# A graph network of four blocks on one core: row fetch on ScalarE's queue, three sums begun early, node types as a product, first operands made in the preparation

## The chip, the cores and the metric

The kernel runs on one core of one Trainium2 chip. The metric is the device time of the whole kernel in microseconds, one launch with all weights read from HBM. Three runs of the kernel before took 1722.24, 1723.06 and 1729.78 us; the median is 1723.06 us.

## What is computed

625 nodes with 768 features, 10625 edges (two directions of 5000 random pairs, and a loop per node), all in float32. Four blocks follow each other, and each one adds to `x` what it computes from `h = max(layernorm(x), 0)`:

```python
# L0: relational mean over 34 edge types, then a GCN layer
mean = agg.reshape(34, n, -1) / max(cnt, 1)
h1 = einsum('rni,rio->no', mean, W_rel) + h @ W_root + b_rgcn
x = x + gcn(h1, W_gcn, b_gcn)
# L1: two GCN layers with relu between
x = x + gcn(relu(gcn(h, W1, b1)), W2, b2)
# L2: three relational layers with 3 edge types; the first has 768 + 128 inputs and 896 outputs
h = concat([h, node_emb[node_type]], -1)          # node_emb is 3 x 128
h = relu(rgcn(h, w_rel1, w_root1, b1)); h = relu(rgcn(h, w_rel2, ...)); h = relu(rgcn(h, w_rel3, ...))
x = x + h
# L3: one GCN layer
x = x + gcn(h, W, b)
```

`gcn` multiplies rows by a weight matrix and sums them over edges with the factor `dinv[src] * dinv[dst]`. `rgcn` multiplies by one matrix for each edge type, sums over the edges of the type, divides by their number, and adds a product with a root matrix.

## The kernel before

**Precision.** Each float32 operand of a large product is held as two fp32r parts, a high one (ScalarE casts it) and a low one (VectorE subtracts the high one from the original), and a product is three matmuls: high by high, high by low, low by high. So each operand passes ScalarE, then VectorE, then TensorE. Nodes lie as 5 tiles of 125 partitions; features as chunks of 128.

**Three programs in a row**, with a barrier of all engines between them (`clear`, L62 to L64):

1. `prepare` sorts the edges by type into units of three tiles of 128 slots, with one-hot matrices on VectorE and matmuls that count on TensorE. Beside that it normalises `x` (`statistics`, L88 and `row_scales`; the activation L1245) and makes `h @ W_root` in 60 float32 matmuls (`root`, L1518), which TensorE works off where its own counting waits: 8, then 4 after each of 5 groups of slots (6 after the last), and so on; what is left runs at the end. ScalarE takes each half tile of them (`take`, L1258), and GpSimd adds them to `sums` in HBM by an indirect DMA (L1221) for four of the five node tiles, and then waits until these have landed. SyncE loads the first unit's weights into `w_raw`.
2. `add_means` runs over some 33 units. Per unit GpSimd gathers rows into `e_raw` (L1895), VectorE makes the matrix `pick` (L2180), ScalarE and VectorE split rows and weights (L1975, L2186, L1979, L2191), TensorE sums (L2328) and multiplies (L2344), ScalarE scales the result (L2014) and GpSimd adds it to `sums` (L1907). In units 6 to 25 the adjacency counts of block L2 are made beside it. After the last unit VectorE adds up the counts of the three edge types (L2246, L2249), then all engines run one pass of a loop that is there for keys with more edges than fit (L2262 and after; PE L2292, L2300). SyncE stores its counts (L1877).
3. `load_rows` and `layers`. SyncE fetches the 625 rows of `sums` in 6 column chunks of 12 DMAs (L128); ScalarE turns the counts into fp32r (`a`, L144), VectorE scales a chunk by `dinv` (L155), ScalarE and VectorE split it. Then come the layers `l0b`, `l1a`, `l1b`, `l21`, `l22`, `l23`, `l3`. A GCN layer is six sums over edges (`edge_sums`, L741, 20 matmuls of 316 columns each) into two banks of PSUM, each then split by ScalarE (L405) and VectorE (L527), and then five products (`products`, L770, 36 matmuls of 384 columns per node tile). A sum may only start in a bank whose sum before has been split (`free`). Between two layers the products' tiles are taken, normalised and split one by one: VectorE L537, L88, L97 to L81, L548; ScalarE L417 casts the high part from `h`; VectorE L559 makes the low part. The next layer's first two sums are begun with four node tiles each and ended with the fifth (`sums_of_all`).

**Layer l21** multiplies 7 feature chunks: 6 of `h` and one of the node type's embedding, which `embeddings()` has written beside `h` in 15 vector instructions. Its rows are turned with 7 transposes per tile (L800), split (L421, L576), and multiplied for 3 edge types and 5 node tiles with 42 matmuls of 448 columns (L770), and for the root matrix with 7 outputs of 42 matmuls of 316 columns (`root_columns`, L845). Weights come through a ring of 4 buffers: the load of a fifth chunk waits until VectorE has split the first (`w_ready`, L520). After the weights of the first edge type, VectorE's program takes and normalises the last tile of l1b (L537 to L554) and then enters `kind_products`, whose first step is L582.

## Time and profile before

| | |
|---|---|
| median of three runs | 1723.06 us |
| the profiled execution | 1722.8 us, of which the span of instructions is 1720.8 us |
| TensorE busy | 95% of the span |
| VectorE, ScalarE, GpSimd | 57%, 36%, 19% |
| mean granted TensorE clock | 0.961 of full |
| DMA | 227.65 MB, 132 GB/s over the span |

The page also cuts the span into 40 slices of 43 us:

```
PE   6987999989999999999498999999999999999988
PEclk7868999999999999999699999999999999999989
DMA  7305997867997789894632131231222212221101
```

Each digit is a busy share in tenths, and PEclk the granted clock in tenths of full speed. The preparation is in the first three to four slices, the means up to slice 19, the layers behind it. A matmul's own duration includes its way through the array, so successive ones overlap; what one costs is read from a run of many, its length divided by their number.

### The profile page before, as it was taken

The numbers are of one execution on the slowest core, as the hardware profiler recorded it, in microseconds if no ns is written. First come the engines' busy times: TensorE is split into PE (matmuls) and PEld (weight loads), VectorE is DVE, ScalarE is ACT, GpSimd is POOL, SyncE is SP. The second block draws the span as 40 slices with busy tenths as digits, with TensorE's granted clock in tenths as the row PEclk, the third lists the DMA queues.
The fourth block names the chain that finished last, engine by engine and source line by source line (L and its number), as shares of the span: only waits on it lengthen the run. The fifth ranks groups of instructions, "written<-read, shape, count | busy, mean of one in ns | idle before, by whom it ended". The sixth has DMA issues, their size and how long they took to land. (4 is left out here: it accounts for less than half of the span.)

```text
span 1720.8 us, 28124 instructions
## 1 busy us (share of the span) xinstructions
PE 1627.5 (95%) x9970; PEld 1510.7 (88%) x9971; DVE 982.0 (57%) x1488; ACT 614.0 (36%) x823; POOL 327.7 (19%) x293
## 2 busy tenths in 40 slices
PE   6987999989999999999498999999999999999988
PEld 4766888879999999988498999999999999999988
DVE  8775997866776676564565474245253442423372
ACT  5104655545665556554222223112231221312220
POOL 0203544543344444342200000000010000000000
PEclk7868999999999999999699999999999999999989
DMA  7305997867997789894632131231222212221101
GB/s 231 90 10 148 258 254 215 241 199 206 271 246 212 211 243 282 250 261 106 106 88 65 42 104 50 63 94 33 56 65 83 75 37 83 74 56 56 55 28 45
DMA packets 97975, 227.65 MB, mean 132 GB/s; under 512 B 11986, under 2 KB 37700, under 8 KB 97898
## 3 DMA queue, kind: packets, MB, share of 16 engines
q1 hardware_dynamic: 72525, 152.19, 27.9%
q0 software_dynamic: 21488, 71.97, 18.7%
q10 hardware_dynamic: 3885, 2.41, 0.5%
q8 instruction: 56, 0.92, 0.2%
q14 instruction: 21, 0.17, 0.0%
HBM read 187.13 MB, written 41.29 MB: 133 GB/s over the span
## 5 line engine op out<-in xcount | busy, mean ns | idle before, releaser
L770 PE MATMUL layers_ps_o<-layers_w_hi,layers_g_hi 128*125 128x384 f32 (+1 forms) x900 | 237.6, 345 | 2.6 <-DVE layers_w_lo L520 2.5
L2344 PE MATMUL l_means_ps<-l_means_w_hi,l_means_g_hi 128*128 128x512 f32 (+1 forms) x912 | 237.8, 342 | 2.1 <-DVE l_means_g_lo L2202 2.0
L770 PE MATMUL layers_ps_o<-layers_w_lo,layers_g_hi 128*125 128x384 f32 (+1 forms) x900 | 237.1, 344 | 0.0
L1979 ACT CAST l_means_w_hi<-w_raw 128x768 fp32r<-128x768 f32 x204 | 170.1, 838 | 187.5 <-PE l_means_ps L2344 168.5
L770 PE MATMUL layers_ps_o<-layers_w_hi,layers_g_lo 128*125 128x384 f32 (+1 forms) x900 | 236.8, 344 | 0.0
L2344 PE MATMUL l_means_ps<-l_means_w_hi,l_means_g_lo 128*128 128x512 f32 (+1 forms) x912 | 235.0, 339 | 0.0
L2344 PE MATMUL l_means_ps<-l_means_w_lo,l_means_g_hi 128*128 128x512 f32 (+1 forms) x912 | 234.1, 338 | 0.0
L2191 DVE TENSOR_TENSOR l_means_w_lo<-w_raw,l_means_w_hi 128x768 fp32r<-128x768 f32 x204 | 186.2, 947 | 69.7 <-ACT l_means_w_hi L1979 60.5
L2328 PE MATMUL l_means_ps<-l_means_pick,l_means_e_hi 128*128 128x256 f32 (+1 forms) x612 | 166.3, 302 | 17.4 <-DVE l_means_e_lo L2186 10.8
L582 DVE TENSOR_TENSOR h_lo<-layers_ps_o,h_hi 125x768 fp32r<-125x768 f32 (+1 forms) x45 | 45.1, 1001 | 238.0 <-ACT h_hi L426 238.0
L741 PE MATMUL layers_ps_g<-a,h_hi 125*128 125x316 f32 x630 | 151.2, 323 | 29.4 <-DVE h_lo L163 12.4
L2344 PEld LDWEIGHTS l_means_ps<-l_means_w_lo,l_means_g_hi 128*128 128x128 f32 x912 | 153.4, 188 | 20.5
L2344 PEld LDWEIGHTS l_means_ps<-l_means_w_hi,l_means_g_hi 128*128 128x128 f32 x912 | 152.0, 189 | 21.6 <-DVE l_means_w_lo L2191 1.8
L2344 PEld LDWEIGHTS l_means_ps<-l_means_w_hi,l_means_g_lo 128*128 128x128 f32 x912 | 153.8, 188 | 19.5
L770 PEld LDWEIGHTS layers_ps_o<-layers_w_hi,layers_g_hi 128*125 128x125 f32 x900 | 162.2, 185 | 7.8 <-DVE layers_w_lo L520 2.9
L1907 POOL DMA_INDIRECT sums<-l_means_y,l_means_row_now x76 | 130.2, 1713 | 201.7 <-ACT l_means_y L2014 173.0
L770 PEld LDWEIGHTS layers_ps_o<-layers_w_hi,layers_g_lo 128*125 128x125 f32 x900 | 163.5, 185 | 4.0
L770 PEld LDWEIGHTS layers_ps_o<-layers_w_lo,layers_g_hi 128*125 128x125 f32 x900 | 163.4, 185 | 3.9
L2328 PE MATMUL l_means_ps<-l_means_pick,l_means_e_lo 128*128 128x256 f32 (+1 forms) x612 | 164.6, 299 | 0.2 <-issue 0.2
L741 PE MATMUL layers_ps_g<-a,h_lo 125*128 125x316 f32 x630 | 149.2, 319 | 0.0
L2202 DVE TENSOR_TENSOR l_means_g_lo<-l_means_ps,l_means_g_hi 128x512 fp32r<-128x512 f32 (+1 forms) x126 | 78.1, 636 | 121.6 <-ACT l_means_g_hi L1993 115.5
L741 PEld LDWEIGHTS layers_ps_g<-a,h_hi 125*128 125x128 f32 x630 | 111.3, 200 | 33.6 <-issue 12.9
(329 smaller groups left out, 2356.7 us busy)
## 6 DMA issues: line engine op xcount, KB each, us to landing
w_raw<-in_L_gnn_W_rel SPq DMA_DIRECT2D x204, 384.0 KB, 6.7
layers_w_raw<-in_L_gnn_w_rel SPq DMA_DIRECT2D x39, 384.0 KB
layers_w_raw<-in_L_gnn_w_rel SPq DMA_DIRECT2D x21, 448.0 KB
layers_a_raw<-adj SPq DMA_DIRECT2D x9, 769.0 KB
layers_w_raw<-in_L_gnn_W SPq DMA_DIRECT2D x18, 384.0 KB
list_now<-targets SPq DMA_DIRECT2D x33, 192.0 KB
layers_w_raw<-in_L_gnn_w_root SPq DMA_DIRECT2D x13, 384.0 KB
layers_w_raw<-in_L_gnn_w_root SPq DMA_DIRECT2D x7, 448.0 KB
```

Of the source, the lines that this page charges most:

```text
L582: v.tensor_tensor(in_halves(h_lo[:, k, 0:layer.width]), out_rows(bank, layer.width), in_halves(h_hi[:, k, 0:layer.width]).bitcast(F32), AL ...
L741: mm = t.matmul(ps_g[:, buf % 2, at:at + PART[p]], rows[:, k, f * 128:(f + 1) * 128], a[:, k, cols], start=(k == 0 and i == 0), stop=(k == ...
L770: mm = t.matmul(ps_o[0:NP, i % 2, a_half, 0:half], g[:, f, at], part_of_w[:, f, a_half * half:(a_half + 1) * half], start=(f == 0 and g is ...
L1907: nc.gpsimd.indirect_dma_start(out=sums, in_=y[:, j, :], in_offset=None, compute_op=ALU.add, out_offset=bass.IndirectOffsetOnAxis(ap=row_n ...
L1979: nc.scalar.copy(w_hi[:, f, :], w_raw[:, f, :]).then_inc(w_hi_ready, 1)
L2191: v.tensor_tensor(w_lo[:, f, :], w_raw[:, f, :], w_hi[:, f, :].bitcast(F32), ALU.subtract)\
L2202: v.tensor_tensor(g_lo[:, f:f + per, at], sums_in_bank(f // per, tiles), g_hi[:, f:f + per, at].bitcast(F32), ALU.subtract).then_inc(g_rea ...
L2328: mm = t.matmul(sums, e[:, j, f * 128:(f + 1) * 128], pick[:, j, 0:cols], start=(j == 0 and part == 0), stop=(j == UNIT - 1 and part == 1))
L2344: mm = t.matmul(ps_y[j][:, o0:o1], g[:, f, at], w[:, f, o0:o1], start=(f == 0 and opens and g is g_hi and w is w_hi), stop=(f == fc - 1 an ...
```

## The change

- **Rows.** SyncE's 12 DMAs (L128) are gone. At the end of `add_means` GpSimd signals `all_added` when the last scatter has landed; ScalarE waits for that and issues 8 DMAs (column chunks 0, 1, 2 to 3, 4 to 5, two partition groups each) from its own queue, still inside `add_means`. `load_rows` casts `a` tile by tile, with the first rows between, and TensorE waits tile by tile; 8 matmuls of a 128 x 128 identity run first (`AWAKE`), and 12 at the end of `add_means` (`LAST_WARM`).
- **Third sum.** GCN layers begin three sums before the fifth tile is there; the third lies in the odd output bank (`gcn_bank`). The fifth tile is split in columns 0 to 255 and the rest. ScalarE computes the high part from `x` with scale and bias (`shift`), beside VectorE's `h`.
- **Node types.** The embedding chunk of `h` becomes 35 columns: one-hot at 0 to 2 and again at 32 to 34. TensorE multiplies the embedding's high and low part by the chunk's weights (`typed_rows`, 6 matmuls for each of 4 weight matrices); ScalarE (`typed_rows_high`) and VectorE (`typed_rows_low`) write high and low parts into `w_lo`, and the chunk's share of a product is one matmul instead of three. Its weights are loaded first, its product comes last, but first for the fifth tile.
- **Preparation.** The statistics of 4 of 5 tiles move to ScalarE (three activations each) and the scales behind the first rank copy; the cast of the diagonal moves to GpSimd; 16 + 4 matmuls keep TensorE busy; 6 instead of 8 root matmuls at first; `pick`, `e_hi`, `e_lo` of unit 0 are made here; GpSimd no longer waits for its scatters, `add_means` waits for all 5. The first unit's weights are loaded later, since their buffer now holds one-hots first.
- **Adjacency.** The adds L2246 to L2249 move from behind the last unit to before the loop of the last units.

```diff
@@ load_rows
-                sp.dma_start(chunk(h[part], f), chunk(rows[part], f)).then_inc(loaded[f], 16)
-        nc.scalar.preload_act_table(ACT.Sqrt)
-        nc.scalar.copy(a[:], adj_all[:]).then_inc(a_ready, 1)
+        copy_counts(0)
+        act.wait_ge(rows_ready, 1)
+        nc.scalar.copy(chunk(h_hi, 0), chunk(h, 0)).then_inc(hi_ready, 1)
+        for k in range(1, NT):
+            copy_counts(k)
...
@@ layers, ScalarE and VectorE
-                    nc.scalar.activation(h_hi[:, k, 0:dim], h[:, k, 0:dim], ACT.Relu).then_inc(layer.hi_ready, 1)
+                    for part in parts_of(k):
+                        nc.scalar.activation(h_hi[:, k, part], x[:, k, part], ACT.Relu, bias=shift[:, k:k + 1],
+                                             scale=rstd[:, k:k + 1]).then_inc(layer.hi_ready, 1)
...
+            if not relu:
+                v.scalar_tensor_tensor(shift[:, at], moments[:, at, 0], -1.0, rstd[:, at], ALU.mult, ALU.mult)\
+                    .then_inc(layer.rows_ready, len(group))
...
+        def typed_rows_high(w):
+            act.wait_ge(typed_summed, typed_number(w) + 1)
+            nc.scalar.copy(in_halves(typed[:, 0:w.width]), typed_bank(w)).then_inc(typed_high, 1)
+        def typed_rows_low(w):
+            n = typed_number(w)
+            dve.wait_ge(typed_high, n + 1)
+            low = in_halves(typed[32:HOT, 0:w.width])
+            v.tensor_tensor(low, typed_bank(w)[32:HOT], low.bitcast(F32), ALU.subtract).then_inc(typed_ready, 1)
...
         def kind_products(layer, r):
+            if layer is l21:
+                typed_rows_low(layer.w[r])
@@ layers, TensorE
+        def typed_rows(w):
+            pe.wait_ge(w_ready, w.first + 1)
+            for i, (e, part_of_w) in enumerate(((0, w_hi), (0, w_lo), (1, w_hi))):
+                for a_half in range(2):
+                    mm = t.matmul(typed_bank(w)[:, a_half, :], emb_parts[e],
+                                  part_of_w[:, w.fc - 1, a_half * half:(a_half + 1) * half], start=(i == 0), stop=(i == 2))
+            mm.then_inc(typed_summed, 1)
...
+                    if by_type and f == w.fc - 1:
+                        pe.wait_ge(typed_ready, typed_number(w) + 1)
+                if by_type and f == w.fc - 1:
+                    terms = ((g_hi[0:HOT, f, at], typed),)
...
+            sums_of_all(layer.w.fc, 3, gcn_bank, free, wait_rows, layer.g_summed)
@@ prepare
-            pool.wait_ge(first_gathered, 16 * UNIT)
-            pool.wait_ge(root_added, 16 * (NT - 1))
-            s.copy(diagonal_keys, diagonal[:].unsqueeze(2).broadcast_to([types, types, EC])).then_inc(diagonal_ready, 1)
+            g.tensor_copy(diagonal_keys, diagonal[:].unsqueeze(2).broadcast_to([types, types, EC])).then_inc(diagonal_ready, 1)
+            for k in range(1, NT):
+                s.activation(h[:, k, 0:width], x[:, k, :], ACT.Copy, accum_out=totals[:, k:k + 1]).then_inc(summed_rows, 1)
...
+                s.activation(h[:, k, 0:width], x[:, k, :], ACT.Square, bias=minus_mean[:, k:k + 1],
+                             accum_out=squares[:, k:k + 1]).then_inc(squared, 1)
...
+            act.wait_ge(first_gathered, 16 * UNIT)
+            for j in range(UNIT):
+                s.copy(e_hi[:, j, :], e_raw[:, j, :]).then_inc(first_split, 1)
...
-            root(8)
+            root(6)
@@ add_means
-            pool.wait_ge(root_added, 16)
+            pool.wait_ge(root_added, 16 * NT)
...
+            act.wait_ge(all_added, 1)
+            for i, (f0, f1) in enumerate(ROW_PARTS):
+                for part in (slice(0, 112), slice(112, NP)):
+                    nc.scalar.dma_start(to[part, :, f0 * 128:f1 * 128], summed_rows[part, :, f0 * 128:f1 * 128])\
+                        .then_inc(second.rows_loaded[i], 16)
```

## Rows read from the trace of the kernel before

**Rows 1.** The page, part 1: TensorE's busy time, share of the span, instructions.

```profile
PE 1627.5 (95%) x9970; PEld 1510.7 (88%) x9971; DVE 982.0 (57%) x1488; ACT 614.0 (36%) x823; POOL 327.7 (19%) x293
```

**Rows 2.** Waits of TensorE by line and releaser: us in total, times, longest us.

```profile
PE layers_ps_g L741 <- DVE h_lo L163: 12.4, 1, 12.4
PE l_means_ps L2328 <- DVE l_means_e_lo L2186: 10.8, 1, 10.8
PE layers_ps_g L741 <- DVE h_lo L559: 8.5, 4, 3.2
...
PE layers_ps_g L741 <- DVE layers_g_lo L527: 6.2, 4, 3.5
PE l_means_ps L2328 <- issue: 5.6, 2, 5.4
```

**Rows 3.** The chain that ended last, in order of time: start us, us, what.

```profile
881.63 19.00 PE layers_ps_o L770 x108
...
924.21 14.61 PE layers_ps_g L741 x80
...
1035.02 8.62 PE layers_ps_o L770 x42
...
1306.79 36.57 PE layers_ps_g L845 x252
```

**Rows 4.** A stage: us, busy us of PE, PEld, DVE, ACT, POOL, PEclk, DMA, GB/s.

```profile
924.20:930.00 5.80, 5.79 (x22) 5.79 (x23) 2.42 (x3) 1.29 (x3) 0.00 (x0) 0.50 0.63 175
```

**Rows 5.** Timeline at the preparation's end: start, us, instruction [idle before <- releaser].

```profile
127.51 1.99 POOL L1221 DMA_INDIRECT sums<-h_rows,node_rows  x1 [31.21 <-ACT h_rows L1258]
...
134.48 0.48 ACT L1258 COPY h_rows<-prep_ps 125x384 f32<-125x384 f32 x1 [3.39 <-PE prep_ps L1518]
...
139.86 1.28 ACT L1969 ACT_TABLE_LOAD   x1 [4.90 <-PEq L64]
...
145.23 0.68 PE L2328 MATMUL l_means_ps<-l_means_pick,l_means_e_hi 128*128 128x384 f32 x1 [10.79 <-DVE l_means_e_lo L2186]
```

**Rows 6.** The instructions of line L1221: time from issue to landing.

```profile
DMA to landing us min/median/max: 9.7/10.4/14.5
```

**Rows 7.** GpSimd: a line's durations (ns min/median/max), and a cast in the timeline.

```profile
L1892 POOL COPY l_means_src_now<-s_src_index x33: 185/317/5081, 145.2 to 771.8; 128x3 int32 x31, 128x3 int32<-128x3 int32 x2
...
848.46 0.29 POOL L135 CAST layers_ones<-layers_ones_f 125x128 fp32r<-125x128 f32 x1
```

**Rows 8.** Timeline at the end of the means, all engines.

```profile
817.83 1.79 DVE L2246 TENSOR_TENSOR adj_all<-l_means_cnt 125x3150 uint16<-125x3150 uint16 x1
...
823.94 0.21 DVE L2262 TENSOR_SCALAR l_means_rank<-l_means_rank 125x85 f32<-125x85 f32 x1 [1.36 <-issue]
...
827.13 0.47 POOL L1900 COPY l_means_row_now<-s_row_index 128x3 int32 x1 [6.11 <-DMA sums<-l_means_y,l_means_row_now]
...
833.73 3.58 PE L2292 MATMUL l_means_ps<-e_raw,l_means_again_slot 125*128 125x240 f16 x17 [4.79 <-DVE e_raw L2157]
...
834.07 1.53 POOL L1907 DMA_INDIRECT sums<-l_means_y,l_means_row_now  x1 [0.30 <-issue]
...
844.63 0.36 SPq L1877 DMA_DIRECT2D adj<-l_means_cnt  x1
```

**Rows 9.** Timeline at the start of the layers.

```profile
848.14 6.65 SPq L128 DMA_DIRECT2D h_rows<-sums  x12
...
849.44 2.82 ACT L144 CAST a<-adj_all 125x3150 fp32r<-125x3150 uint16 x1
...
855.84 0.87 PE L741 MATMUL layers_ps_g<-a,h_hi 125*128 125x316 f32 x2 [12.43 <-DVE h_lo L163]
```

**Rows 10.** Timeline: VectorE's low part of the fifth tile behind l0b.

```profile
920.72 0.96 DVE L559 SCALAR_TENSOR_TENSOR h_lo<-h_rows,h_hi 125x768 fp32r<-125x768 f32 x1 [0.91 <-ACT h_hi L417]
```

**Rows 11.** Timeline at the start of l21: TensorE's seventh chunk, VectorE's L582.

```profile
1032.78 0.67 PE L770 MATMUL layers_ps_o<-layers_w_hi,layers_g_hi 128*125 128x448 f32 x2 [0.74 <-DVE layers_w_lo L520]
...
1037.57 1.08 DVE L582 TENSOR_TENSOR h_lo<-layers_ps_o,h_hi 125x896 fp32r<-125x896 f32 x1
```

384 lines of the change are left out of this document (250 added, 134 removed).

## Prediction

> **What bounds the kernel now.** First the page's busy times: TensorE is busy 95% of the span [rows 1], so a gain is either matmuls that go or the 5% in which it waits, together with the slow clock behind such waits. Then TensorE's waits by releaser [rows 2]. They are few and long: 12.4 us before the layers' first sum, 10.8 us before the first unit, 8.5 us for normalised tiles, 6.2 us for a freed bank. Then the chain of waits, for what one matmul costs back to back at full clock [rows 3]: 19.00 / 108 = 0.176 us with 384 columns, 8.62 / 42 = 0.205 with 448, 36.57 / 252 = 0.145 with 316. Last the granted clock: it stood at 0.50 (1.2 GHz of 2.4) for 5.8 us from 924.2 on, behind two waits [rows 2, 4]. Its four sums of 80 matmuls took 14.61 us [rows 3] where 80 x 0.145 = 11.6 would do, so such a pair of waits costs 3.0 us beyond itself.
>
> All terms are against the profiled execution: 1722.8 us, a span of 1720.8 us and 2.0 us around it. The median of the runs is 0.3 us higher, so I use the same number for both.
>
> **1. Preparation and first unit.** GpSimd issues its fourth scatter at 127.51 [rows 5], and it lands 9.7 to 14.5 us later [rows 6]. That is about 138, and the barrier opens at 139.86, though ScalarE's last take ends at 134.96 [rows 5]. Without the wait the takes set the end. Two root matmuls more stand at the tail, about 1.3 us, and the chain before it is about 1.2 us shorter (root(6) lets the slot counts go 1.2 us earlier, and VectorE loses four tiles of statistics), so the end stays near 135.2 and the block opens at about 136.1: -3.75. ScalarE's 12 new activations lie in a stretch where it waited; VectorE's pick and e_lo of unit 0 lie beside the tail of root matmuls, which hides them. TensorE started its first unit at 145.23, 5.4 us after the block opened [rows 5], because pick, e_hi and e_lo came first. These are made already, so it can start about 1.3 us after. ScalarE's and VectorE's splits of the weights, which stood behind them, become late next: the sixth sum waits about 0.7 us for them. That leaves -3.15. Sum **-6.9**, bounds -3 (splits and first gather late) and -8. The means run on TensorE, so the shift should stay.
>
> **2. Adjacency adds.** The adds and the entry to the pass take VectorE from 817.83 to 823.94 [rows 8]. Before the loop of the last units they hold up VectorE's split of the next unit's first sums: about 5 us of work against the 4.2 us that TensorE's sums last. **+0.5**, bounds 0 and +2.
>
> **3. End of the means and l0b.** TensorE's part of the pass started at 833.73 after 4.79 us of waiting for VectorE [rows 8]. Without the adds it starts when the last unit is done and its loop is entered, about 830.5, and the store of the counts (844.63) comes out near 839.5. Now ScalarE is late next. The last scatter is issued at 834.07 to 835.6; the one before it held GpSimd 6.1 us after its issue [rows 8], so `all_added` comes at about 841.9. Eight DMAs at 0.45 us (12 took 5 to 6.65 us on SyncE [rows 9]) are 3.7 us more, and a barrier of 0.9 us follows: the layers open at about 846.8 instead of 848.14. **-1.3**, bounds +1.5 and -4.
> In the layers TensorE began 7.7 us after the opening, at 855.84 [rows 9]: DMA, scaling, a 2.8 us cast of all counts [rows 9], two splits. Now the first rows have landed before the block, and scaling, cast and split of one chunk are 3 x 0.8 us: it starts at +2.6. The weights of l0b no longer queue behind 12 row DMAs, so the 3.5 us wait of the third sum [rows 2] goes, and a third bank lets ScalarE and VectorE lag one sum. VectorE's 24 steps of some 0.77 us are then 18.5 us from +0.1, about as long as the six sums, 6 x 20 x 0.147 = 17.6. With 1.8 us at the slow clock and 0.3 us of small waits the products start at +22.3, where before they started at 881.47 (six matmuls ahead of the chain's piece at 881.63 [rows 3]), +33.3. **-11.0**, bounds -6 (rows or weights land late, slow clock) and -14.
>
> **4. Third sum and split behind a normalisation.** Behind l0b: per tile VectorE loses the 0.91 us wait for ScalarE [rows 10] and gains the shift (0.2 us) and a smaller wait, -0.46 per tile. Over tiles 2 to 4, with the fifth in two parts, the first part of the last tile is ready at about 919.5 instead of 921.7. TensorE has 48 matmuls (7.0 us) until 920.1 instead of 32, so its waits of 0.4 and 3.2 us go, the wait for a bank shrinks from 1.0 to 0.5, and the slow clock's 3.0 us go with them [rows 2 to 4]: the sums end at 931.2 instead of 938.8, **-7.6**, bounds -4.5 and -8. Behind l1a only a part of one bank wait (1.3 us) goes: **-0.85**. Behind l23 VectorE's tile takes longer than TensorE's product, so it stays late: waits of 2.2, 2.7 and 0.6 us become about 1.4, 0.8 and 0.8, and half the slow clock stays: **-5.7**, bounds -3 and -7.5.
>
> **5. Node types (l21).** Removed: 4 of 42 matmuls in 15 products, 60 x 0.205 = 12.3 us, and 28 x 0.145 = 4.1 us in the root. Added: 24 typed matmuls, 4.9 us. For edge types 1 and 2 all of it counts, since the splits of the typed rows hide behind 36 matmuls of the first tile: 2 x (1.23 - 4.1) = -5.7. Edge type 0 is another matter. Its weights come in at VectorE's pace, the last chunk at 1032.78 [rows 11], so the first tile ends its six plain chunks at about 1034.0. Its typed product then waits for `typed_rows_low`, which in VectorE's program stands behind the last tile's normalisation, where L582 stood, at 1037.57 [rows 11]. 1.08 us for it, taken from L582's row of the same width: 1038.7. **A new wait of 4.7 us**, and the slow clock behind it, 2.2 us (less than the 3.0 above). Against that stand 3 x 0.82 us of tiles 1 to 3. Tile 4 and the root's first output are paced by VectorE's reciprocal and splits, which shift along, with a second wait of about 1 us for the root's typed rows and 0.9 us of other waits and slow clock; then six outputs save 0.58 us each. Type 0 and root together: 4.7 + 2.2 + 0.35 (the later chunk order) - 2.45 + 1.9 - 3.5 = +3.2. Sum **-2.5**, bounds -8 (typed rows in time) and +3 (slow clock twice).
>
> Embedding loads (GpSimd's two DMAs), 35 columns instead of 128, SyncE's later load of the first weights (its buffer is free at about 82, needed at 137) and the warming matmuls cost nothing: they lie where the engine has nothing due.
>
> **Sum:** -6.9 + 0.5 - 1.3 - 11.0 - 7.6 - 0.85 - 5.7 - 2.5 = -35.35. 1722.8 - 35.35 = **1687.5 us**.
>
> **Rivals.**
> (a) The typed rows come in time, or the clock does not fall behind them: term 5 is -9. 1681 us. Against it: the order in VectorE's program.
> (b) The rows' early fetch brings little. ScalarE issues it so late that block and rows come as before, and only the smaller cast and the third bank count: terms of part 3 are +1 and -6. 1694 us. For it: the estimate has the fetch only 6 us ahead of the old one, and ScalarE holds the barrier.
> (c) GpSimd's cast of 2890 columns blocks VectorE's compare of the types (L1299), which all of the preparation waits for. At 0.29 us for 128 columns [rows 7] it takes 4 to 6.5 us from 2.7 on, and the compare began at 5.5: +1.5 to +3.8, 1690 us. The rows show the other direction only: a copy of three columns on GpSimd took 185 ns to 5081 ns [rows 7]. The Trainium skill, "SBUF — State Buffer", section "Who interferes with whom", says that a VectorE instruction with two inputs in SBUF and a GpSimd one that reads SBUF exclude each other for a whole instruction, and the first to start wins. By that rule the cast wins here, and the time is that of (c); the trace agrees as far as GpSimd's waits go, and has no long GpSimd instruction that could show VectorE waiting.
> (d) Slower than before. TensorE once waited 5.4 us in the means for nothing that the profile shows [rows 2], on entering a new loop. If that is the loading of its program, the change, which adds branches to straight code of the layers and another order to each program, could bring more such pauses. With the slow clock one costs 5.4 + 2.2 = 7.6 us; from five new ones on the gain of 35 is gone: 1724 us and above. Against it: the layers' code, straight already, shows no such wait.
>
> **Chances.** Forecast (1681 to 1694 around 1687.5) 0.58; (a) 0.13; (b) 0.15; (c) 0.08; (d) 0.02; the rest, 0.04, lies between 1700 and 1723. The range must reach (a), (b) and (c) with the bounds of the large terms: 1676 to 1700. About 0.5% is what a measurement can tell from no change. Faster by over 0.5% (below 1714.4) 0.95, within 0.5% 0.03, slower 0.02.
>
> **What the changed profile would show.** The means' first matmul at about 137.4; ScalarE's row DMAs from about 835 (842 less the shift of 6.4); TensorE's first sum 2.6 us after the layers open and the products 22 us after; no wait over 1 us between the products of l0b and l1a; a wait of 4 to 5 us for `typed_ready` in the first tile of l21 and a clock of 0.50 behind it; the count of 448-column matmuls on L770's line down by 60, with 24 typed ones on a line of their own. I would be wrong by much if the means absorbed the early start, which a first matmul at 137 with an unchanged end of the means would show, or if the rows' DMAs were issued after the barrier's other engines had come.

## The result and the profile after

The changed kernel takes 1708.1 us (1701.5 to 1709.1) against 1724.0 us, a ratio of 0.988 (95% interval 0.986 to 0.991). It is faster, by less than half of what was forecast (1687.5, range 1676 to 1700). In the profiled executions the span went from 1720.8 to 1707.2 us, 13.6 less, where the sum had 35.4. Two executions beside these, one of 4007.7 us in `fetch_sync` below and one of 2369.7 us of the kernel before, are left out of all times and ratios. The page, part 1:

```profile
PE 1628.4 (95%) x9954; PEld 1498.6 (88%) x9955; DVE 981.2 (57%) x1486; ACT 626.3 (37%) x858; POOL 333.3 (20%) x297
```

There are 16 matmuls fewer than in [rows 1], and the busy time is the same. So what is gained is waiting, and not much of it. The waits of TensorE, after (line and releaser: us in total, times, longest):

```profile
PE l_means_ps L2497 <- issue: 18.3, 5, 7.0
PE layers_ps_o L1019 <- PEq L64: 6.6, 1, 6.6
PE prep_ps L1684 <- DMA prep_root_w<-in_L_gnn_W_root: 5.9, 1, 5.9
...
PE layers_ps_o L871 <- DVE layers_w_lo L644: 4.6, 1, 4.6
...
PE l_means_ps L2513 <- DVE l_means_g_lo L2373: 3.6, 2, 2.7
PE layers_ps_g L821 <- DVE h_lo L626: 2.5, 2, 1.9
PE layers_ps_g L821 <- DVE layers_g_lo L591: 2.4, 4, 0.7
```

Against [rows 2]: the 12.4 us for the first rows' low part are a 6.6 us wait for the block; 8.5 and 6.2 us for normalised tiles and a freed bank are 2.5 and 2.4. Those parts did what they should. New are 18.3 us of "issue" where there were 5.6, and waits for the root weights (2.6 before), for `g_lo` and for the typed rows. By stages, each bounded by the same matmuls in both traces:

| stage | us before | after | forecast | measured |
|---|---|---|---|---|
| A: to the first matmul of the means | 145.2 | 144.3 | -6.9 | -0.9 |
| B: means, to the end of the last unit | 683.5 | 692.1 | +0.5 | +8.5 |
| C: to l0b's products | 52.9 | 40.7 | -12.3 | -12.2 |
| D: to the end of l1a's sums | 57.2 | 50.1 | -7.6 | -7.1 |
| E: to the end of l1b's sums | 50.5 | 49.9 | -0.85 | -0.6 |
| F: l21, to l22's root | 317.5 | 321.8 | -2.5 | +4.3 |
| G: to l3's products | 374.2 | 367.9 | -5.7 | -6.3 |
| H: to the end | 39.8 | 40.4 | 0 | +0.7 |

C, D, E and G are within 0.6 us of the forecast. A, B and F hold 20.8 of the 21.8 us that are missing. The 0.7 us that part 1 of the forecast gave to late splits fall into unit 0 and so into stage B.

One profile of each kernel says less of A and F than of the rest. Over all the profiled executions below, the means began at 144.4 to 147.6 us in four with the preparation of before, and at 141.7 to 144.4 in eight with the changed one: some 3 us earlier on average, not 0.9. Stage F took 316.6 to 319.4 us in those four and 319.3 to 322.6 in the ten that keep the changed l21.

### The profile page after: what moved, and what is told of

Read it like the earlier page. It is cut to its first block and busy times, and to the rows that moved or that the text cites. A ratio compares the mean times of both kernels' runs of the same rounds, so it can differ in the third digit from the quotient of the medians.

```text
span 1707.2 us, 28150 instructions
## 1 busy us (share of the span) xinstructions
PE 1628.4 (95%) x9954; PEld 1498.6 (88%) x9955; DVE 981.2 (57%) x1486; ACT 626.3 (37%) x858; POOL 333.3 (20%) x297
## 3 DMA queue, kind: packets, MB, share of 16 engines
q0 software_dynamic: 21552, 71.98, 18.7%
## 5 line engine op out<-in xcount | busy, mean ns | idle before, releaser
L871 PE MATMUL layers_ps_o<-layers_w_lo,layers_g_hi 128*125 128x384 f32 (+2 forms) x900 | 239.4, 347 | 4.6 <-DVE layers_w_lo L644 4.6
L871 PE MATMUL layers_ps_o<-layers_w_hi,layers_g_hi 128*125 128x384 f32 (+1 forms) x870 | 230.5, 346 | 0.8 <-DVE layers_w_lo L584 0.8
L871 PE MATMUL layers_ps_o<-layers_w_hi,layers_g_lo 128*125 128x384 f32 (+1 forms) x870 | 228.6, 344 | 0.0
L2497 PE MATMUL l_means_ps<-pick,e_hi 128*128 128x256 f32 (+1 forms) x612 | 167.7, 304 | 18.8 <-issue 18.3
L871 PEld LDWEIGHTS layers_ps_o<-layers_w_lo,layers_g_hi 128*125 128x125 f32 (+1 forms) x900 | 162.7, 186 | 12.4 <-DVE layers_w_lo L644 4.9
L2497 PE MATMUL l_means_ps<-pick,e_lo 128*128 128x256 f32 (+1 forms) x612 | 165.6, 300 | 0.0
L871 PEld LDWEIGHTS layers_ps_o<-layers_w_hi,layers_g_hi 128*125 128x125 f32 x870 | 156.5, 186 | 8.5 <-issue 3.4
L821 PE MATMUL layers_ps_g<-a,h_hi 125*128 125x316 f32 x590 | 136.0, 312 | 7.1 <-DVE h_lo L626 2.5
L2497 PEld LDWEIGHTS l_means_ps<-pick,e_hi 128*128 128x128 f32 x612 | 119.7, 196 | 22.1 <-issue 19.8
L2064 POOL DMA_INDIRECT e_raw<-rows,l_means_src_now x99 | 127.0, 1283 | 49.5 <-POOL l_means_src_now L2061 27.2
```

Of the source, the lines that this page charges most:

```text
L821: mm = t.matmul(to[:, at:at + PART[p]], rows[:, k, f * 128:(f + 1) * 128], a[:, k, cols], start=(k == 0 and i == 0), stop=(k == NT - 1 and ...
L871: mm = t.matmul(ps_o[0:NP, i % 2, a_half, 0:half], g, part_of_w[:, a_half * half:(a_half + 1) * half], start=(f == order[0] and n == 0), s ...
L2064: nc.gpsimd.indirect_dma_start(out=e_raw[:, j, :], out_offset=None, in_=rows, in_offset=bass.IndirectOffsetOnAxis(ap=src_now[:, j:j + 1], ...
L2497: mm = t.matmul(sums, e[:, j, f * 128:(f + 1) * 128], pick[:, j, 0:cols], start=(j == 0 and part == 0), stop=(j == UNIT - 1 and part == 1))
```

## Where the three stages lost it

**Preparation (A).** Its end and the first matmul of the means, after (timeline: start, us, instruction, [idle before <- releaser]):

```profile
137.33 0.48 ACT L1409 COPY h_rows<-prep_ps 125x384 f32<-125x384 f32 x1 [3.39 <-PE prep_ps L1684]
142.41 1.28 ACT L2139 ACT_TABLE_LOAD   x1 [4.60 <-PEq L64]
...
144.33 0.68 PE L2497 MATMUL l_means_ps<-pick,e_hi 128*128 128x384 f32 x1 [7.04 <-issue]
```

ScalarE's last take ends at 137.81 and the block opens 4.60 us later. In [rows 5] it was 134.96 and 4.90 us. The row's releaser, TensorE's sequencer (PEq L64), only takes part in the barrier. What comes last is GpSimd's fourth scatter, still, though the program no longer waits for it (timeline, and time from issue to landing):

```profile
130.36 1.99 POOL L1367 DMA_INDIRECT sums<-h_rows,node_rows  x1 [29.55 <-ACT h_rows L1409]
...
DMA to landing us min/median/max: 10.6/10.6/10.6
```

It lands at 140.94, and the block opens 1.47 us behind that. The trace has GpSimd's closing DRAIN, the instruction with which it leaves the block, from 130.11 to 141.28: it ends 0.34 us behind the landing. So the wait that was removed stands in this instruction as well. In the kernel before the scatter landed at 137.87 and the block opened 1.99 us behind it.

And the takes end 2.85 us later than before, not 0.2. TensorE's start in the preparation, after:

```profile
34.40 6.89 PE L1684 MATMUL prep_ps<-prep_root_w,prep_root_g 128*125 128x384 f32 x12 [5.88 <-DMA prep_root_w<-in_L_gnn_W_root]
41.13 2.91 PE L1694 MATMUL prep_ps<-prep_is_tile,w_raw 125*128 125x186 f16 x34
...
44.08 1.29 DVE L1526 TENSOR_TENSOR prep_is_slot<-prep_iota,prep_slot_of 125x2176 f16<-125x2176 f16 x1 [6.61 <-PE prep_ps L1694]
```

The same in the kernel before:

```profile
33.60 5.42 PE L1518 MATMUL prep_ps<-prep_root_w,prep_root_g 128*125 128x384 f32 x16 [2.60 <-DMA prep_root_w<-in_L_gnn_W_root]
```

VectorE was 4.1 us ahead at its first one-hots (26.4 against 30.5), but TensorE reached `root` sooner only to wait longer for its weights, which land at 34.4 instead of 33.6. After 5.88 us of idling its 12 root matmuls take 0.57 us each, before 16 took 0.34 (the trace shows each of the kernel's 6 and 8 as two). The slot counts, for which VectorE and all behind it wait, begin at 41.1 instead of 38.9. Both times vary: the weights landed at 33.0 to 34.3 in the four executions of before and at 33.5 to 34.6 with the changed preparation, the takes ended at 134.3 to 137.3 and at 135.3 to 138.0. So the lead of 4.1 us is lost in each of them, and of the 2.85 us about 1 is the change, by the averages, and the rest differs from execution to execution.

**Means (B).** Time from the first matmul of one unit to that of the next, units counted from 0, for all those that differ by over 0.5 us:

| unit | 0 | 2 | 3 | 5 | 6 | 7 | 10 | 11 | 26 | 30 |
|---|---|---|---|---|---|---|---|---|---|---|
| before | 26.8 | 17.6 | 17.9 | 25.3 | 19.8 | 18.7 | 24.4 | 20.4 | 17.3 | 17.7 |
| after | 27.8 | 21.5 | 16.9 | 27.4 | 25.4 | 20.5 | 18.8 | 18.1 | 21.5 | 16.9 |

Unit 26 is the one beside which VectorE does the adjacency adds now. After:

```profile
673.27 1.12 DVE L2415 TENSOR_TENSOR adj_all<-adj_all,ident 125x125 uint16<-125x125 uint16 x5
...
676.66 0.69 DVE L2373 TENSOR_TENSOR l_means_g_lo<-l_means_ps,l_means_g_hi 128x512 fp32r<-128x512 f32 x1 [2.27 <-ACT l_means_g_hi L2161]
...
677.48 0.61 PE L2513 MATMUL l_means_ps<-l_means_w_hi,l_means_g_hi 128*128 128x512 f32 x2 [2.72 <-DVE l_means_g_lo L2373]
```

The adds begin at 669.61. ScalarE's half (`g_hi`) had been there since 674.07, before the adds ended: the 2.27 us between them and `g_lo` are VectorE's own, in which the trace shows it load bounds from memory, enter the loop and branch. I had counted the adds, 5 us against 4.2, and not the entry. TensorE waits 2.7 us and the unit costs 4.2 us.

The other units hold pauses of TensorE for which the profile names nothing. After:

```profile
193.77 0.58 PE L2497 MATMUL l_means_ps<-pick,e_hi 128*128 128x256 f32 x1 [2.73 <-issue]
...
273.41 0.38 PE L2497 MATMUL l_means_ps<-pick,e_hi 128*128 128x256 f32 x1 [1.92 <-issue]
...
298.76 0.58 PE L2497 MATMUL l_means_ps<-pick,e_hi 128*128 128x256 f32 x1 [6.40 <-issue]
```

Before:

```profile
368.61 0.58 PE L2328 MATMUL l_means_ps<-l_means_pick,l_means_e_hi 128*128 128x256 f32 x1 [5.41 <-issue]
```

The one of before, in front of unit 11, is gone, and three others are there: in unit 2, and in front of units 6 and 7. By the kernel, units 2, 6, 11 and 26 are the first of a loop of TensorE's, and unit 7 is the second pass of one. Units 2 to 11 together cost 4.4 us more. In these pauses the DMA view shows the queue that carries instructions at work. After, 292.5 to 298.7 (packets, MB, share of 16 engines):

```profile
q8 instruction: 2, 0.03, 1.9%
```

and before, 363.3 to 368.6:

```profile
q8 instruction: 1, 0.02, 1.2%
```

The changed kernel's second execution (below) has no pause in front of unit 7. From the start of unit 6 to that of unit 7 the same row reads, in the first (273.5 to 298.7) and in the second (270.7 to 289.3):

```profile
q8 instruction: 4, 0.07, 0.9%
...
q8 instruction: 2, 0.03, 0.6%
```

Two packets fewer, and no pause. Elsewhere such packets move without one, at 378.8 and 387.0 for instance.

**l21 (F).** The wait for the typed rows came where it was forecast, for 4.56 us, and the granted clock of 1025 to 1030 was 0.51, that is 1.2 GHz of 2.4:

```profile
1023.94 1.08 DVE L644 TENSOR_TENSOR layers_w_lo<-layers_ps_g,layers_w_lo 3x896 fp32r<-3x896 f32 x1
...
1025.08 1.10 PE L871 MATMUL layers_ps_o<-layers_w_lo,layers_g_hi 35*125 35x448 f32 x2 [4.56 <-DVE layers_w_lo L644]
...
1025.00:1030.00 5.00, 4.92 (x16) 4.08 (x17) 2.06 (x3) 1.85 (x3) 0.00 (x0) 0.51 0.00 0
```

That part was right. What was not is the saving. Typed matmuls within an undisturbed tile, TensorE's matmuls and its weight loads (PEld), after:

```profile
1148.62 0.56 PE L871 MATMUL layers_ps_o<-layers_w_hi,layers_g_lo 128*125 128x448 f32 x2
1149.11 0.67 PE L871 MATMUL layers_ps_o<-layers_w_lo,layers_g_hi 35*125 35x448 f32 x2
1149.71 0.68 PE L871 MATMUL layers_ps_o<-layers_w_hi,layers_g_hi 128*125 128x448 f32 x2
1150.23 0.56 PE L871 MATMUL layers_ps_o<-layers_w_lo,layers_g_hi 128*125 128x448 f32 x2
...
1149.11 0.29 PEld L871 LDWEIGHTS layers_ps_o<-layers_w_lo,layers_g_hi 35*125 35x125 f32 x2 [0.30 <-issue]
1149.71 0.29 PEld L871 LDWEIGHTS layers_ps_o<-layers_w_hi,layers_g_hi 128*125 128x125 f32 x2 [0.31 <-issue]
```

A pair of 128-row matmuls stands 0.40 us behind the last one. Into and out of the pair with 35 rows it is 0.49, 0.60 and 0.52: the weight load starts 0.30 us late both times, where loads of equal rows run on without a gap. A tile of 36 plain and 2 typed matmuls takes 8.22 us (1140.89 to 1149.11), where 38 x 0.205 is 7.8. Against the 8.62 us of [rows 3] that saves 0.40 us per tile, half of the 0.82 forecast.

## The experiments

All kernels compute the full result. In the expectations a pause "at unit 11" is the one in front of it. Theory A, in the three runs after the first, is the account above. The changed kernel itself once more, to see what repeats:

> The changed kernel once more, nothing edited. Its first profile shows TensorE paused four times in the means with nothing that the profile shows ahead of it (2.7 us in the third unit, 1.9 before the seventh, 6.4 before the eighth, after 7.0 before the first), where the kernel before had one such pause (5.4 us, before the twelfth unit). Theory P (place): the pauses belong to places of TensorE's program, which the change has shifted, and come back at the same units with about the same lengths; the unit from 172.1 us on and the loop of the keys repeat within 0.2 us. Theory R (chance): they belong to what the DMA engines carry in that execution; they lie at other units or have lengths that differ by microseconds, and the whole time moves with their sum. Time 1701 to 1709 us by both.

1707.0 us (1694.7 to 1709.5), ratio 0.990. The profiled execution took 1694.7 us, the others 1705 to 1710. It had the pauses of units 2 and 6 (theory P) but not that in front of unit 7, and so spent 664.6 us from the first matmul to unit 33 instead of 675.0. It also had its first matmul at 141.87, so 2.5 us of stage A vary between executions. I compare stages and not only times below.

**Typed rows at full height.** The same number of matmuls, with 128 rows, the unused ones zero:

```diff
-                    terms = ((g_hi[0:HOT, f, at], typed),)
+                    terms = ((g_hi[:, f, at], w_lo[:, f, :]),)
-                        terms = ((typed[:, out_chunk], g_hi[0:HOT, f, :]),)
+                        terms = ((w_lo[:, f, out_chunk], g_hi[:, f, :]),)
```

> Node types: the chunk of the node type stays one matmul instead of three, but with all 128 rows (rows 35 to 127 of the left operand are zero) instead of 35. In the changed kernel a tile of l21 took 8.22 us for 38 matmuls, where 38 x 0.205 = 7.8 were forecast; before and behind each pair with 35 rows 0.50 and 0.60 us pass instead of 0.41. Theory B: the cost lies in the chunk's place or its own operand (the typed rows in the low weights): a tile stays at 8.2 us and the time at the changed kernel's.

1698.1 us, ratio 0.984 (0.981 to 0.987). l21 took 312.4 us instead of 321.6, 9.2 less (and 7 to 10 less than in the other executions that keep the changed l21), and a tile 7.76 us:

```profile
1143.68 0.57 PE L871 MATMUL layers_ps_o<-layers_w_lo,layers_g_hi 128*125 128x448 f32 x2
...
1151.44 0.56 PE L871 MATMUL layers_ps_o<-layers_w_lo,layers_g_hi 128*125 128x448 f32 x2
```

So the forecast's price of a matmul was right, and what it left out is the price of changing the number of rows. Shown.

**Adds behind the loop of the last units** (ahead of the last unit):

```diff
+            with dve.Fori(lead_units + key_units, last_unit(dve)) as n:
+                one_unit(unit(n))
             for t in range(1, second.kinds):
                 then(v.tensor_tensor(flat, by_type[:, 0, :] if t == 1 else flat, by_type[:, t, :], ALU.add))
...
             then(ins)
-            with dve.Fori(lead_units + key_units, last_unit(dve)) as n:
-                one_unit(unit(n))
```

> VectorE's five additions of the counts stand between the loop of the last units and the last unit instead of ahead of the loop. In the changed kernel they end at 674.4 us, VectorE then needs 2.3 us to enter the loop, TensorE waits 2.7 us for the first low part and the unit takes 21.45 us instead of 17.3. Theory A: it is the sum of additions and loop entry that costs; where VectorE is through with the loop and would wait 4.5 us for ScalarE anyway, they cost 0 to 1 us: the unit at 670 us takes 17.3 us again, the last unit is later by at most 1 us, and the kernel is 3 to 4 us faster than the changed one. Theory B: the additions cost the same wherever they stand ahead of the last unit, since VectorE has no slack for 5 us: the loss of 4 us moves to the last unit and the time stays.

1702.0 us, ratio 0.986 (0.984 to 0.989). Unit 26 took 17.47 us, 4.0 less than in the changed kernel. But in the last unit, unit 33, TensorE now waits for VectorE, which comes from the adds:

```profile
818.23 0.69 DVE L2373 TENSOR_TENSOR l_means_g_lo<-l_means_ps,l_means_g_hi 128x512 fp32r<-128x512 f32 x1 [1.76 <-ACT l_means_g_hi L2161]
...
819.05 0.61 PE L2513 MATMUL l_means_ps<-l_means_w_hi,l_means_g_hi 128*128 128x512 f32 x2 [1.57 <-DVE l_means_g_lo L2373]
```

That unit took 19.0 us instead of 17.15, so about half of the gain comes back: 4.0 - 1.8 = 2.2 us stay. Stage B took 690.2 us, against 691.9 to 692.6 in five executions that have the same pauses and the adds ahead of the loop. The truth lies between theories A and B.

**Slot counts ahead of the root products:**

```diff
-            root(6)
             for n in range(EC // chunk):
                 slots(n)
-                root(4 if n < EC // chunk - 1 else 6)
+                root((0, 6, 6, 6, 10)[n])
```

> Preparation: TensorE's six first root matmul pairs, which wait for the root weights, stand behind the first group of slots instead of ahead of it (6, 6, 6 and 10 behind groups 2 to 5, none behind the first). In the changed kernel VectorE has the first one-hots ready 4.1 us earlier than before (26.4 instead of 30.5 us), but TensorE stands 5.9 us for the root weights, which land at 34.4, works six pairs off at half clock and comes to the slots at 41.1, later than before (38.9); VectorE then stands 6.6 us at 44.1. Theory A: the wait for the root weights and the clock behind it ate the lead: now the first slots run at 32 to 33 us, VectorE's 6.6 us go, and every step behind, down to the first unit, comes 4 to 6.5 us earlier (first unit at 138 to 140.5 instead of 144.3). Theory B: something else sets the end of the preparation (the root matmuls themselves, 20.5 us of them, or the stores of the rows): the first unit stays within 1.5 us of 144.3.

1695.2 us, ratio 0.984 (0.982 to 0.986). The 12 root matmuls, now behind the slot counts and their weights landed, run at full clock:

```profile
40.36 4.06 PE L1684 MATMUL prep_ps<-prep_root_w,prep_root_g 128*125 128x384 f32 x12
...
133.45 0.48 ACT L1409 COPY h_rows<-prep_ps 125x384 f32<-125x384 f32 x1 [3.39 <-PE prep_ps L1684]
138.30 1.28 ACT L2138 ACT_TABLE_LOAD   x1 [4.38 <-PEq L64]
```

The takes end 3.9 us earlier and the first unit starts at 140.19, 4.1 us before that of the changed kernel and 1.7 before its repeat. All five kernels with this order started it at 140.0 to 141.6, the eight with the changed preparation at 141.7 to 144.4: the order is worth about 2 us. The median is 12 us below the changed kernel's, more than the order explains: the profiled execution also lacks the pause in front of unit 7 (665.0 us from the first matmul to unit 33). Whether the order has a part in that is open.

**The kernel before once more, and two attempts at moving code.** Theory P, from here on: a pause belongs to a place in TensorE's program, and so moves with the number of instructions ahead of it. Ahead of the means' code stand 848 matmuls in the kernel before and 868 in the changed one (its 20 new warming matmuls), if each of the 60 root matmuls, two in the trace, is counted once.

> The kernel before once more, nothing edited, for its pauses. In its profile TensorE has one pause over 1 us with nothing ahead of it in the means (5.4 us before the twelfth unit) and none in the third, seventh or eighth unit. Theory P (place): the same again, possibly without the long one. Theory R (chance): pauses of 2 to 6 us at other units, as the changed kernel has them. First unit at 145.2 us within 1 us, the last unit ended near 829 less the 5.4 us and their slow clock where the pause is absent. Time 1721 to 1727 us.

> The changed kernel with 64 empty instructions in TensorE's program of the preparation, where TensorE waits for the normalised rows anyway (13 to 22 us), so that all of its program behind them lies 64 instructions later. Nothing else. Theory P (place in the program's memory): the pauses of 2 to 4 us in the third unit and 2 us before the seventh change or move to other units, and the means take another time by some microseconds. Theory S (structure): the pauses hang on the loops themselves (first pass of a loop, entry of the next), not on where the code lies; they stay at the third, seventh and eighth unit. The two halves of a unit repeat at 16.92 and 8.4 us by both.

> The kernel before with 40 empty instructions in TensorE's program of the preparation, where it waits for the normalised rows anyway. 40 is what the change adds to that program (20 warming matmuls, two instructions each). Theory P (place in the program's memory): the pauses of the changed kernel appear here too: unit 2 takes 20 to 21.5 us instead of 17.4 to 17.6, 2 us before unit 6, and the long one at unit 7 or 11. Theory S (something else in the change): the units take what they take in the kernel before, with the one pause of 5.4 to 5.8 us at unit 11.

The kernel before took 1724.0 us, ratio 0.9997, with its pause of 5.8 us again in front of unit 11. The other two had `t.nop()` 64 and 40 times ahead of the means and came out as their unedited kernels, in time (ratios 0.988 and 0.999) and pauses. But the traces, which also list what TensorE's sequencer does, hold the same instructions ahead of the means as without the edit and none of the empty ones. So these were most likely never in the programs, and the two runs are repeats that say nothing on P.

**GpSimd's waits back, at the end of its preparation:**

```diff
                     .then_inc(root_added, 16)
+            pool.wait_ge(first_gathered, 16 * UNIT)
+            pool.wait_ge(root_added, 16 * (NT - 1))
```

> GpSimd waits again at the end of the preparation until the four scatters of the root rows have landed. Theory A, the prediction's: this wait held the barrier before (it opened 4.9 us behind ScalarE's last take), so it opens 2 to 4 us later than without it. Theory B: GpSimd was never the last; TensorE's sequencer is the last at the barrier and the gap of 4.4 to 4.6 us behind the last take stays as it is, within 0.5 us.

1709.8 us, ratio 0.991. The number is that of theory B:

```profile
136.50 0.48 ACT L1411 COPY h_rows<-prep_ps 125x384 f32<-125x384 f32 x1 [3.39 <-PE prep_ps L1686]
141.77 1.28 ACT L2141 ACT_TABLE_LOAD   x1 [4.79 <-PEq L64]
```

From take to opening 4.79 us with the waits, 4.60 and 4.48 without. The reason is not that of theory B. Measured from the landing of the fourth scatter, at 139.76 here, the opening comes 2.0 us later in all five kernels with the waits and 1.47 in all fifteen without. GpSimd was the last in all twenty, whether it stood in the wait or in its DRAIN. Taking the wait out of the program brought 0.5 us, not 3.75. No run took the scatter itself off the path.

**Typed rows prepared ahead of l21**, in both engines' programs:

```diff
         w_high(l21.w[0], f)
+        typed_rows_high(l21.w[0])
...
                     w_low(l21.w[0], f)
+                typed_rows_low(l21.w[0])
             take(l1b, k)
```

> Node types, first edge type: ScalarE and VectorE split the typed rows right behind the seventh chunk of weights, ahead of the last tile's normalisation, not behind it. In the changed kernel VectorE does it at 1023.9, TensorE has waited 4.6 us for it and then runs 4.8 us at half clock; the last weights are split at 1019.0. Theory A (the prediction's): the typed rows are ready at about 1020.1, TensorE's wait goes to under 1 us, the half clock behind it goes, and the rest is earlier by 4.6 + 2 = 6.5 us; at most 1 us of it is lost again at the root's weights, which stand behind VectorE's reciprocal. Theory B: VectorE is late next in any case, since the last tile's normalisation is 1.1 us later and the splits of the first products with it: TensorE waits at tile 2 or at the root, and less than 3 us are gained.

1692.9 us, ratio 0.981 (0.978 to 0.983). VectorE's L644 (L645 there) starts at 1017.71 and no longer holds TensorE; l21 takes 314.8 us, 6.8 less. The forecast had 4.7 + 2.2 for this wait and the slow clock behind it. The median is lower by more than that, 14 us; the profiled execution, the slowest of the six with 1700.7 us, has the pause in front of unit 7, and some of the others probably lack it, but they have no trace.

**Warming matmuls undone** (`WARM` 16 to 12, `WARM_ROWS` 16 to 0: TensorE's program ahead of the means is again as long as before):

> The changed kernel without the 20 warming matmuls that it added in the preparation (12 instead of 16, 0 instead of 16), so that TensorE's program ahead of the means is 40 instructions shorter. Theory P (place): the pauses at units 2, 6 and 7 go and one of 5.4 to 5.8 us stands at unit 11, as in the kernel before; the means are 5 to 8 us shorter, and up to 2 us of it are lost to a slow clock in the preparation. Theory S: the pauses stay at units 2, 6 and 7.

1704.3 us, ratio 0.987 (0.984 to 0.989), and

```profile
369.21 0.57 PE L2497 MATMUL l_means_ps<-pick,e_hi 128*128 128x256 f32 x1 [5.61 <-issue]
```

The pauses at 2, 6 and 7 are gone, that in front of unit 11 is back. From the first matmul to unit 33 it took 671.3 us; the changed kernel took 675.0, or 664.6 without the pause at 7.

**The same the other way:** 20 tiny matmuls (two columns) ahead of the means of the kernel *before*, and 108 in the changed kernel, which with its own 20 is 128 matmuls more than before. Each matmul is two instructions (a weight load and the product), so this is 256 instructions.

```diff
+            for i in range(20):
+                t.matmul(bank[:, sums_bank, 0:2], ones[:], ones[:, 0:2], start=True, stop=True, skip_group_check=True)
             pe.wait_ge(placed, 1)
```

> The kernel before with 20 tiny matmuls (two columns each, into a bank that is free) in TensorE's program of the preparation, where it waits for the normalised rows; empty instructions don't reach the program, matmuls do. The changed kernel has 868 matmuls ahead of the means, the kernel before 848, this one 868. Theory P (place in the program): units 2, 6 and 7 take 20 to 21.5, 27 and 25 us as in the changed kernel (17.6, 25.3 and 19.8 in the kernel before), and the pause at unit 11 is gone. Theory S (something else in the change): the units are as in the kernel before, one pause of 5.4 to 6 us at unit 11.

 Theory P16 (it is the place within such a transfer that decides): the pauses of the kernel before and of the changed kernel without its 20 warming matmuls come back: one of 5.4 to 6 us at unit 11, none at units 2, 6 and 7. Theory P' (place matters, with another period): pauses at yet other units. Theory S: as the changed kernel, units 2, 6, 7.

Kernel before with 20 of them, 1728.2 us, ratio 1.002 (1.0002 to 1.004):

```profile
195.52 0.38 PE L2330 MATMUL l_means_ps<-l_means_pick,l_means_e_hi 128*128 128x256 f32 x1 [3.25 <-issue]
...
274.73 0.38 PE L2330 MATMUL l_means_ps<-l_means_pick,l_means_e_hi 128*128 128x256 f32 x1 [1.84 <-issue]
...
301.56 0.58 PE L2330 MATMUL l_means_ps<-l_means_pick,l_means_e_hi 128*128 128x256 f32 x1 [6.36 <-issue]
```

Changed kernel with 108, 1702.7 us, ratio 0.987 (0.985 to 0.990):

```profile
368.50 0.58 PE L2499 MATMUL l_means_ps<-pick,e_hi 128*128 128x256 f32 x1 [5.36 <-issue]
```

The kernel before has the changed one's three pauses, and the changed one that of the kernel before. So the pauses follow the place of the loops in TensorE's program, with a period that 256 instructions fit, and not the change's other parts. The Trainium skill, "Runtime: NRT & Kernel Launch", section "Instruction fetch mechanics", says that an engine's instructions are fetched in blocks of 16 KiB (256 instructions), which mostly hides behind work, and that a taken branch whose target isn't held forces a fetch. The traces agree so far as they go: the packets have 16 KB, the last of them starts 2.4 to 3.4 us before the end of each pause shown, and the pauses stand in or in front of the first or second unit of a loop. That the loops' branches are the trigger rests on this rule; no run took a loop apart.

**Rows fetched by SyncE again**, from the layers' block, the rest of the change kept:

```diff
-                    nc.scalar.dma_start(to[part, :, f0 * 128:f1 * 128], summed_rows[part, :, f0 * 128:f1 * 128])\
-                        .then_inc(second.rows_loaded[i], 16)
...
+    @block.sync
...
+                sp.dma_start(h[part, :, f0 * 128:f1 * 128], rows[part, :, f0 * 128:f1 * 128]).then_inc(loaded[i], 16)
```

> The changed kernel with the 8 transfers of the rows issued by SyncE in the layers' block again; everything else, the counts cast tile by tile and the third bank among it, stays. Changed kernel: 17.8 us from the last unit's end to the opening of the layers, first sum 3.45 us behind the opening, products of l0b 23.0 us behind it. Theory A (the prediction's: early rows are worth most of part 3): the layers open 2.5 to 3.8 us earlier, the first sum comes 6 to 7 us behind the opening, the products 25 to 27 us behind it, and the sum of all is 0 to 1.5 us later: of the 10 us that the layers' start gained, the early fetch has at most 1.5, the rest is the cast in parts, the weights ahead of fewer transfers and the third bank. Theory B: the fetch itself is the gain: products 30 us behind the opening and the kernel 5 us slower.

1709.7 us (1705.7 to 1721.0, three executions), ratio 0.989 (0.986 to 0.992), which doesn't set it apart from the changed kernel (0.988). Its stages do, and against what I had expected:

```profile
857.00 3.83 SPq L126 DMA_DIRECT2D h_rows<-sums  x8
861.40 18.36 SPq L384 DMA_DIRECT2D layers_w_raw<-in_L_gnn_W_gcn  x6
...
865.11 0.89 PE L828 MATMUL layers_ps_g<-a,h_hi 125*128 125x316 f32 x2 [4.30 <-DVE h_lo L173]
...
878.59 0.89 PE L828 MATMUL layers_ps_g<-a,h_hi 125*128 125x316 f32 x2 [3.02 <-DVE layers_g_lo L598]
```

The same stretch of the changed kernel:

```profile
847.79 3.83 ACTq L2212 DMA_DIRECT2D h_rows<-sums  x8
...
854.15 3.75 PE L1019 MATMUL layers_ps_o<-ident 128*128 128x128 f32 x16 [6.61 <-PEq L64]
854.45 1.78 SPq L377 DMA_DIRECT2D layers_w_raw<-in_L_gnn_W_gcn  x4
```

From the start of unit 33 to l0b's products it is 67.1 us against 57.8. The block opens 18.0 us behind the last unit, as in the changed kernel (17.7), so ScalarE's transfers don't hold it. GpSimd's DRAIN does again: it takes 5.3 us in both (850.72 to 856.05 here, 847.83 to 853.15 in the changed kernel, where ScalarE is through at 851.92), and the opening follows 1.0 us behind. All scatters have landed by then; why it takes 5.3 us stays open. The first sum comes 8.1 us behind the opening instead of 3.5, and the weights of l0b queue again behind the rows, with 3.0 us of waiting. So the early fetch is worth 9.4 of stage C's 12.2 us.

**`LAST_WARM` 12 to 0:**

> The changed kernel without the 12 warming matmuls at the end of the means. In the changed kernel they end at 847.55, and the layers open at 854.1, 6.6 us behind them, while ScalarE issues the last row transfer at 851.2; with the rows fetched by SyncE behind the opening, the gap behind them was 6.8 us and the opening no earlier. In the kernel before TensorE's last matmul ended at 843.4 and the opening was 4.7 us behind. Theory A (TensorE is the last at this barrier): without them the layers open 2 us earlier, limited then by ScalarE's transfers, and the products of l0b start 1 to 2 us earlier, with up to 1 us lost to a slower clock in the first sum. Theory B (ScalarE is the last): the opening stays within 0.5 us (17.8 us behind the last unit's end) and the products are late by the slow clock, 1 to 2 us.

1703.7 us, ratio 0.989. From unit 33 to the warming matmuls of the next block 35.3 us (34.8 with them), to the products 58.3 (57.8). The 12 matmuls neither delay the block nor bring anything that can be seen.

**The edits together:** full rows, adds later, typed rows early and slots first, then with the warming matmuls undone, and with the warming matmuls and 44 or 76 tiny ones ahead of the means (64 and 96 matmuls more than in the kernel before, counted with the 20).

> Four edits together on the changed kernel: node type chunk with 128 rows, typed rows split ahead of the last tile's normalisation, additions of the counts between the last units' loop and the last unit, first slots ahead of the root matmuls. Alone they took 9.2 us and 6.8 us off the stage of l21, 4 us off the unit at 670 us and 1.6 to 4 us off the preparation. Theory A (they lie in different stages and add up): 22 to 24 us under the changed kernel, 1684 to 1687 us. Theory B (node types: with the first tile free of its wait, VectorE's reciprocal and the splits of the root's weights are late next, and the two edits of l21 share their gain): 1689 us or more.

> The four edits together, and TensorE's code of the means at the place where the kernel before has it (848 matmuls ahead of it, without the 20 warming ones). By the place theory: units 2, 6 and 7 at 17.4, 25.3 and 20.1 us, one pause of 5.4 to 5.6 us at unit 11, so the means are 3.7 us shorter than with the changed kernel's place where that has all three pauses: 1685 us or a little under (best_1: 1689.1), with a smaller spread from run to run. If the place were not the cause, the pauses would be those of best_1.

> The four edits with 44 tiny matmuls ahead of the wait for the normalised rows: 912 matmuls ahead of the means, 64 more than the kernel before, half of the 128 after which the pattern came back. Open which units pause; by the place theory it is neither the pattern of the kernel before (11) nor that of the changed kernel (2, 6, 7). If the theory is only that few matmuls matter, one of those two comes back. Sum of the pauses 0 to 15 us, time 1680 to 1695.

> The same with 76 tiny matmuls, 96 more than the kernel before. Open as well, for the same reason: a third pattern, or one of the three that the other places give. Whatever it is, the units outside the pauses repeat at 17.96, 18.7, 16.92 and 26.3 us. Time 1680 to 1695.

1689.1 us with the changed kernel's place (ratio 0.977, 0.975 to 0.979); 1684.4 with the place of before (0.977, 0.975 to 0.978); 1685.1 with 64 (0.977) and 1693.7 with 96 (0.982, 0.981 to 0.984). Where each met its own runs of the kernel before, the first three can't be told apart by their ratios. The edits of l21 add up: it took 306.3 us, 15.3 less than in the changed kernel where 9.2 and 6.8 make 16.0. No place is free of pauses: with 64 TensorE pauses 1.25 us at 366.2 and 5.10 at 663.0, with 96 it pauses 5.17 us at 366.6 and 5.50 at 668.8.

The change with the typed rows at full height and prepared early, the adds behind the loop and the slot counts first is thus 2.3% below the kernel before, where the change alone is 1.2%. Without the new warming matmuls it is no slower.

## Why the prediction was wrong, step by step

**Part 1** failed in three steps. The first matmul came at 144.3, forecast 137.4, 6.9 us late. (i) "Without the wait the takes set the end": they didn't. I had read [rows 5 and 6] rightly, the fourth scatter held the barrier, but it holds it without the program's wait too, because GpSimd's DRAIN lasts until the scatter has landed. The block opens 4.6 us behind the last take where I had 0.9, 3.7 us. (ii) The takes end at 137.8 instead of 135.2, 2.6 us, of which over 1 us is this execution's and not the change's. I moved `root` and `slots` with VectorE's 1.2 us and did not ask when the root weights land. (iii) The first matmul comes 1.9 us behind the opening, not 1.3; that it comes so much sooner than the 5.4 us of before, 3.5 us less, is the part of the term that held. Unit 0 took 1.0 us longer, forecast 0.7, but mostly not for late splits: 0.7 us of it lie in its first 18 matmuls, since the granted clock was still 0.50 from 3.0 to 4.4 us behind the start, where before it had been 0.91. Two sums of mine were also slightly off: 5.4 - 1.3 - 0.7 is 3.4 and not 3.15, and in part 3 the opening adds up to 846.4, not 846.8.

**Part 2**: +4.2 us, forecast +0.5 with +2 as bound. The step that failed is the work beside TensorE's sums: the loop entry of 2.3 us was left out of it. Before, VectorE's adds and its entry lay in the pass behind the units; the 1.36 us of "issue" in [rows 8] is such an entry and was the row to take.

**Part 3**: -12.2, forecast -12.3. Within it two errors cancel: `all_added` came 11.4 us behind the last unit, where I had 13.1, and the block opened 6.3 us after the first row DMA, where I had 4.6 with ScalarE as the last. GpSimd was, with the 5.3 us of its DRAIN. That gap was 6.3 us without `LAST_WARM` too. First sum 3.5 us behind the opening (2.6), products 23.0 (22.3).

**Part 4**: -7.1 (-7.6), -0.6 (-0.85), -6.3 (-5.7). Its method, one wait after another down the tiles of a stage and the slow clock with them, held.

**Part 5**: +4.3, forecast -2.5. The wait (4.56 for 4.7) and the clock behind it (6.8 together for 6.9) were right. The price of the typed matmuls was mis-sized: 0.40 us saved per tile and not 0.82, 0.19 per root output and not 0.58, and edge types 1 and 2 gave 0.8 us each and not 2.9. That is 4.1 + 1.3 + 2.3 = 7.7 us; the waits around tile 4 and the root were about 0.9 us smaller. I had taken a duration from matmuls of one shape and used it for two shapes in turn. The Trainium skill, "TensorE: Matmul & The Clock Gate", section "Step-by-step: what each phase is for", says that the time of loading the weights grows with their columns, and that the number of rows doesn't matter. For the load alone the trace agrees, 0.29 us for a pair of 35 rows and for the pair of 128 behind it; it says nothing of a change from one number to the other, which here costs 0.4 us per pair.

**Rivals.** (a) and (b) fell by their stages: the typed rows were late, and the early fetch brought 9.4 us. (c) fell: GpSimd's long instruction and VectorE's cast of the keys did meet,

```profile
2.65 2.58 POOL L1347 COPY prep_early<-prep_diagonal 34x2890 f16<-34x2890 f16 x1
...
3.98 1.60 DVE L1451 CAST prep_key<-prep_raw 125x85 f16<-125x85 int32 x1 [3.86 <-DMA prep_raw<-in_edge_type]
```

and the cast took 1.60 us where it had been 0.21, but VectorE waited for ScalarE behind it in both kernels, and the compare began at 5.62 instead of 5.47. (d) named the cause of the means' loss, pauses while TensorE's program is fetched, and its price per pause was near (6.4 us and a slow unit behind it, for 7.6). But I made it depend on the layers' straight code and on five pauses, gave it 0.02 and nothing of it to the sum. The layers' code moved no pause. Twenty matmuls ahead of a loop did, and it cost 4.4 us in the profiled execution. The range should have held one such pause more or less, some 7 us either way.

## What to carry to other kernels

Before you book a removed wait as a gain, ask whether the end of the block waits for the same thing anyway, and when the data of the work that moves up will land: here these two were 6.3 of the 21.8 us that I had too much. Measure from the landing of a transfer to the opening of the block: a distance that stays the same to 0.01 us over many executions names what came last, where one gap allows several readings. Keep one number of rows through a run of matmuls; zeros that fill the partitions are cheaper than a short pair. Where one engine runs large loops, every instruction added ahead of them moves them against the fetching of its program, so compare two kernels stage by stage and look for pauses with no releaser before a difference of some 5 us is put down to the edit.
